# Columns loaded by halves, an identity kept in the transposed matrix, and VectorE's order: one core

## The chip, the cores and the metric

The kernel runs on 1 core of a Trainium2 chip. Its time is the device time of one execution, in microseconds (us). The engines are TensorE (PE in the profile, its weight loads PEld), VectorE (DVE), ScalarE (ACT), GpSimd (POOL) and SyncE (SP), which here only issues transfers. Each runs its own instructions in the order in which they are written, and waits on semaphores for the others.

## The reference

For each of 16 graphs there are `x` (1024 nodes x 256) and a weighted adjacency matrix `adj` (1024 x 1024). Four layers follow each other, each `x = layernorm(x + f(x, adj))`. Layer 0 touches 25 nodes a graph. The others, cut to what matters:

```python
# layer 1: attention
z = x @ W.T + bW;  e = leaky(ai(z) + aj(z).T, 0.2)
x = layernorm(x + softmax(where(adj > 0, e, -9e15), with a sink) @ z)
# layer 2
h = (1.0 + eps2) * x + adj @ x
x = layernorm(x + relu(h @ W1 + b1) @ W2 + b2)          # hidden 512
# layer 3
agg = eps3 * x + adj @ x
h = rmsnorm(agg @ W1 + b1) * rms_weight                  # hidden 1024
x = layernorm(x + silu(h) @ W2 + b2)
```

## The kernel before

A prologue (`prologue`) loads the weights and computes layer 0. Then `layers` takes the graphs one by one, and parts of the next graph's work are laid between those of the present one. Nothing is scheduled by a planner: every engine has a function `graph(b, ...)` whose text is its order. 1024 nodes are 8 tiles `k` (or `t`) of 128 and two halves `h` of 512. Where precision matters a float32 matrix is held as a sum hi + lo of two tiles of the type fp32r, and a product takes three matmuls: hi by hi, hi by lo, lo by hi.

- `agg_step(layer, k, h)` (L662 to L679) adds the contribution of node tile k to half h of the aggregate: 3 matmuls of 512 columns for each of two halves `d` of the features, 6 in all. The moving operand is the transposed matrix `mt_hi`, `mt_lo`: in layer 1 the attention weights (from `att`), in layers 2 and 3 the adjacency matrix. 16 such steps make a layer.
- The transposed adjacency matrix is made from column blocks. ACT issues `load_col` (L850): 1024 rows of 128 columns, 512 KB, into one of two slots of `adj_col` (`CR` = 2), after it has read the block before from that slot's transpose. POOL adds eps3 times the identity to the block's own 128x128 piece (`diagonal`, L1031). PE transposes it by 8 matmuls with the identity into two PSUM banks (`turn_col`, L638), ACT copies to `mt_hi` (`turn_hi`, L847), DVE subtracts to get `mt_lo` (`turn_lo`, L1095) and so frees the banks.
- Since eps3 is on that diagonal, layer 2 needs 1 + eps2 - eps3 more: in `agg_step` with `extra`, 3 matmuls of 128 columns with the tiles `cI2_hi`, `cI2_lo` for each `d` (L675 to L677).
- `attention_out` (L698) multiplies by W, `hidden_tile` (L713) by the first and `second_step` (L729) by the second weight matrix, `agg_hi` (ACT, L878) and `agg_lo` (DVE, L1109) take the aggregate out of PSUM as `a_hi`, `a_lo`. `residual`, `statistics`, `normalize` (DVE, L1120/L1125, L1137 to L1145, L1152) with `rstd_of` (POOL, L1009), `x_high` (ACT, L882) and `x_low` (POOL, L1014) are the way from a layer's output to the next layer's operand, by halves.
- `rms_sum` (L741) and `rms_row` (L753) on PE, with `mean_square` (L1219) and `rms_of` (L1035), make layer 3's norm. The second half of layer 3's second matmul (L729, 8 steps `m`) is done after half 0 of the next graph's layer 1.
- Attention weights of graph b + 1 are computed on DVE while PE is in layers 2 and 3 of graph b: `attention_sums` (L1160), `attention_columns`, `aj_rows` on PE (L649), `aj_copy` (L1102), then 8 times `scores` (mask L1182, L1184, L1189), each followed by `exp` on ACT (L886); `denominators` end it, and then `turn_att` (L629) transposes `att` on PE.
- SP stores the finished graph, loads the next one's `x` tiles and, once `att` has been transposed, its 8 rows of `adj` into `att` (512 KB each).

## Time and profile before

| | us |
|---|---|
| median of 3 runs (3111.78 to 3113.38) | 3112.48 |
| the profiled execution's own time | 3113.45 |
| its span on the chip | 3111.7 |
| PE busy | 2895.0 (93%) |
| DVE busy | 2082.6 (67%) |
| ACT busy | 1323.5 (43%) |
| POOL busy | 923.3 (30%) |

Busy time counts an engine's instructions, not its waits. Successive matmuls overlap in the profile, since the end of one is modelled: what a stream of them costs is read from start to start. "Idle before" is the time that an engine sat still before an instruction, and behind the arrow stands what ended it.

### The profile page before, as it was taken

What the parts mean: (1) busy time and instruction counts of PE and PEld (TensorE: products, weight loads), DVE (VectorE), ACT (ScalarE), POOL (GpSimd) and SP (SyncE); (2) the same over time, 40 slices, a digit from 0 to 9 for tenths busy, and PEclk for the clock granted to TensorE, in tenths of its full rate; (3) what the DMA queues carried; (4) which work ended last, traced back from release to release, by engine and by line L of the source; (5) the groups of instructions that cost most, each with busy time, mean ns of one, the idle gap of its engine ahead of it and who ended that gap; (6) DMA issues with size and microseconds to landing.
All of it is one profiled execution on the core that took longest, in us unless ns stands there. A gap on an engine that the chain in (4) does not pass through costs nothing.

```text
span 3111.7 us, 40093 instructions
## 1 busy us (share of the span) xinstructions
PE 2895.0 (93%) x14794; PEld 2438.7 (78%) x14794; DVE 2082.6 (67%) x4580; ACT 1323.5 (43%) x2468; POOL 923.3 (30%) x1088
## 2 busy tenths in 40 slices
PE   4729999999999999999999999999999999999997
PEld 4618888888888888888888888888888888888886
DVE  3277667685867758586776858676676858677533
ACT  0222634436253543535254453526344362635423
POOL 1113333242233224223322323233332422332230
PEclk8959999999999999999999999999999999999998
DMA  4023040211304030130403012040302103040100
GB/s 131 15 79 115 1 129 7 80 57 36 100 1 136 1 109 28 41 95 1 136 1 116 21 49 88 3 133 1 126 10 76 60 28 109 1 136 1 41 15 14
DMA packets 203442, 180.95 MB, mean 58 GB/s; under 512 B 15568, under 2 KB 184944, under 8 KB 203248
## 3 DMA queue, kind: packets, MB, share of 16 engines
q1 hardware_dynamic: 62560, 109.94, 10.3%
q10 hardware_dynamic: 140688, 68.46, 7.8%
q8 instruction: 118, 1.93, 0.3%
q14 instruction: 76, 0.62, 0.1%
HBM read 161.17 MB, written 17.19 MB: 57 GB/s over the span
## 4 chain that ended last, share of the span: by engine, by line
PE 77%; DVE 10%; ACT 3%; POOL 3%; issue 2%; DMA 0%; SPq 0%; ACTq 0%; POOLq 0%; DVEq 0%
PE bank L729 21%; PE bank L713 17%; PE bank L670 9%; PE bank L672 9%; PE bank L671 9%; PE bank L629 3%; PE bank L638 3%; DVE mt_lo L1095 3%; DVE stat L1137 2%; PE bank L698 2%; POOL x_lo L1014 2%; PE bank L753 1%; PE bank L741 1%; PE bank L649 1%; ACT mt_hi L847 1%
## 5 line engine op out<-in xcount | busy, mean ns | idle before, releaser
L729 PE MATMUL bank<-W,hid 128*128 128x256 f32 x3072 | 695.3, 380 | 5.9 <-ACT hid L922 5.9
L729 PEld LDWEIGHTS bank<-W,hid 128*128 128x128 f32 x3072 | 583.3, 190 | 97.5 <-issue 12.7
L670 PE MATMUL bank<-mt_hi,x_hi 128*128 128x512 f32 x1536 | 642.1, 418 | 0.0
L672 PE MATMUL bank<-mt_hi,x_lo 128*128 128x512 f32 x1536 | 606.0, 395 | 0.0
L671 PE MATMUL bank<-mt_lo,x_hi 128*128 128x512 f32 x1536 | 603.4, 393 | 0.0
L847 ACT ACTIVATE mt_hi<-bank 128x512 fp32r<-128x512 f32 x512 | 279.7, 600 | 583.2 <-PE bank L638 547.7
L1009 POOL TENSOR_TENSOR rstd<-ve,neg_half 128x4 f32<-128x4 f32 x128 | 130.2, 1017 | 908.3 <-DVE ve L1145 908.2
L1215 DVE TENSOR_TENSOR sq_sum<-sq_sum,scratch 128x512 f32<-128x512 f32 x224 | 155.1, 692 | 360.6 <-ACT scratch L917 360.6
L1095 DVE TENSOR_TENSOR mt_lo<-bank,mt_hi 128x512 fp32r<-128x512 f32 x512 | 329.8, 684 | 88.0 <-ACT mt_hi L847 86.2
L672 PEld LDWEIGHTS bank<-mt_hi,x_lo 128*128 128x128 f32 x1536 | 290.8, 189 | 65.5
L713 PE MATMUL bank<-a_hi,W_hi 128*128 128x512 f32 x768 | 332.1, 432 | 0.0
L670 PEld LDWEIGHTS bank<-mt_hi,x_hi 128*128 128x128 f32 x1536 | 292.8, 191 | 48.0 <-ACT scratch L917 4.2
L671 PEld LDWEIGHTS bank<-mt_lo,x_hi 128*128 128x128 f32 x1536 | 293.0, 191 | 44.6
L713 PE MATMUL bank<-a_hi,W_lo 128*128 128x512 f32 x768 | 303.6, 395 | 0.0
L713 PE MATMUL bank<-a_lo,W_hi 128*128 128x512 f32 x768 | 302.8, 394 | 0.0
L1014 POOL TENSOR_TENSOR x_lo<-x_even,x_hi 128x256 fp32r<-128x256 f32 x192 | 167.9, 885 | 286.1 <-ACT x_hi L882 286.1
L908 ACT ACTIVATE hid<-bank,b 128x512 f32<-128x512 f32 x256 | 176.0, 688 | 165.0 <-PE bank L729 127.1
L1014 POOL TENSOR_TENSOR x_lo<-x_odd,x_hi 128x256 fp32r<-128x256 f32 x192 | 165.8, 874 | 258.9 <-ACT x_hi L882 258.9
L886 ACT ACTIVATE att<-att,neg_top 128x1024 f32<-128x1024 f32 x128 | 147.1, 1151 | 211.3 <-DVE neg_top L1196 211.0
L922 ACT ACTIVATE hid<-hid 128x512 f32<-128x512 f32 x256 | 161.8, 632 | 160.9 <-DVE hid L1226 157.1
L1109 DVE TENSOR_TENSOR a_lo<-bank,a_hi 128x512 fp32r<-128x512 f32 x192 | 123.5, 685 | 153.5 <-ACT a_hi L878 153.5
L878 ACT ACTIVATE a_hi<-bank 128x512 fp32r<-128x512 f32 x192 | 103.1, 588 | 253.3 <-PE bank L672 253.3
(139 smaller groups left out, 4609.6 us busy)
## 6 DMA issues: line engine op xcount, KB each, us to landing
adj_col<-in_adj ACTq DMA_DIRECT2D x128, 512.0 KB, 3.9
att<-in_adj SPq DMA_DIRECT2D x128, 512.0 KB, 7.5
out<-x_even SPq DMA_DIRECT2D x64, 128.0 KB, 2.5
out<-x_odd SPq DMA_DIRECT2D x64, 128.0 KB, 1.9
x_even<-in_x SPq DMA_DIRECT2D x56, 128.0 KB, 4.9
x_odd<-in_x SPq DMA_DIRECT2D x56, 128.0 KB, 4.2
G<-in_L_gnn_W SPq DMA_DIRECT2D x2, 2560.0 KB, 14.8
W_f<-in_L_gnn_W SPq DMA_DIRECT2D x1, 1024.0 KB, 9.8
```

The source lines that it names most:

```text
L670: nc.tensor.matmul(dst[:], hi, mt_hi[:, k, cols], start=k == 0, stop=False)
L671: nc.tensor.matmul(dst[:], hi, mt_lo[:, k, cols], start=False, stop=False)
L672: mm = nc.tensor.matmul(dst[:], lo, mt_hi[:, k, cols], start=False, stop=done and not extra)
L713: mm = nc.tensor.matmul(hid_bank[i % 2][:], l[:, d, cols], r[:, d, :], start=(d == 0 and n == 0), stop=(d == DT - 1 and n == 2))
L729: mm = nc.tensor.matmul(out_bank[t // 2][:, t % 2 * D:(t % 2 + 1) * D], src[:, t * P:(t + 1) * P], W2[:, m, :], start=(m == 0 and t % 2 == ...
L847: nc.scalar.activation(mt_hi[:, k, i * HALF:(i + 1) * HALF], turn_bank[i][:], ACT.Copy)\
L886: nc.scalar.activation(att[:, t, :], att[:, t, :], ACT.Exp, bias=neg_top[:, t:t + 1], accum_out=total[:, t:t + 1]).then_inc(s_exp, 1)
L908: nc.scalar.activation(hid[:, m, :], src, ACT.Identity, bias=b13[:, m:m + 1])
L922: nc.scalar.activation(h_m, h_m, ACT.Silu).then_inc(s_silu, 1)
L1014: nc.gpsimd.tensor_tensor(x_lo[:, t, :], x_bufs[buf][:, t, :], x_hi[:, t, :].bitcast(F32), ALU.subtract).then_inc(s_x_lo, 1)
L1095: nc.vector.tensor_tensor(mt_lo[:, k, cols], turn_bank[i][:], mt_hi[:, k, cols].bitcast(F32), ALU.subtract).then_inc(s_turn_free[i], 1)
L1215: nc.vector.tensor_tensor(sq_sum[:], sq_sum[:], sq[:, m % 2, :], ALU.add).then_inc(s_sq_sum, 1)
```

## The change

Four things are done together.

1. `adj_col` gets a place for the whole matrix and lies in the same memory as `mt_lo`: a half block (k, h), 512 rows of 128 columns and 256 KB, is loaded into the place of `mt_lo[k, h]` once layer 1's step (k, h) has used it. SP issues these loads, 16 a graph, between its stores and loads. `turn_col(b, k, h)` transposes a half block (4 matmuls, one bank, the two banks by turns). Six of them stand in the loop of `second_step`, five in layer 1's half 1 (`COL_AT`), five in layer 2.
2. The diagonal now carries 1 + eps2 (`cI2`), and the matmuls L675 to L677 are gone. For layer 3 the 8 diagonal pieces are rewritten: DVE keeps each, plus (eps3 - 1 - eps2) times the identity, in `diag3`; once layer 2's half is summed, ACT writes the hi part (`diag_hi`) and POOL the lo part (`diag_lo`), 4 pieces in one instruction each.
3. `agg_done` is signalled for each `d`, and steps 6 and 7 of layer 3's half 1 are done first for d = 0, then for d = 1. `rms_sum` of half 1 has a bank of its own.
4. The orders of PE, ACT, POOL and DVE are rewritten to suit, and `score_mask` is cut out of `scores`.

```diff
     x_hi, x_lo = sb("x_hi", [P, NT, D], F32R), sb("x_lo", [P, NT, D], F32R)
     a_hi, a_lo = sb("a_hi", [P, DT, HALF], F32R), sb("a_lo", [P, DT, HALF], F32R)
@@ -484,12 +486,13 @@
 
     agg_pair = [banks[0:2], banks[2:4]]
     hid_bank = banks[0:2]
-    sum_bank, row_bank = banks[6], banks[2]
...
+
+    COL_AT = {0: (6, 0), 1: (7, 0), 4: (0, 1), 5: (1, 1), 6: (2, 1)}
...
+            def load_col(b, k, h):
+
+                if k < NT - 1:
+                    sp.wait_ge(s_att_used, used_count(b, k, h))
+                else:
+                    sp.wait_ge(s_agg, DT * agg_count(b, 1, h))
+                dst = adj_col[:, k, half_cols(h)].rearrange("p (t m) -> p t m", t=4)
+                src = adj[b, half_cols(h), k * P:(k + 1) * P].rearrange("(t p) m -> p t m", p=P)
+                sp.dma_start(dst, src).then_inc(s_col_in[k][h], 16)
...
+                for k in range(NT - 1):
+                    load_col(b, k, 0)
                 if not first:
...
+                load_col(b, NT - 1, 0)
+                if not last:
+                    load_xs(b + 1, tiles(0), 1 - buf, first)
                     sp.wait_ge(s_turned[1], turn_att_use(b, NT - 1) + 1)
                     for t in range(4):
                         load_row(b + 1, t)
+                for k in range(4):
+                    load_col(b, k, 1)
                 if not first:
                     for t in tiles(1):
...
+                for k in range(4, 6):
+                    load_col(b, k, 1)
+                if not last:
+                    load_xs(b + 1, tiles(1), 1 - buf, first)
+                for k in range(6, NT):
+                    load_col(b, k, 1)
...
+            def turn_col(b, k, h):
+                if k // 4 == h:
+                    pe.wait_ge(s_diag, b * NT + k + 1)
+                else:
+                    pe.wait_ge(s_col_in[k][h], (b + 1) * 16)
+                i = col_bank(k, h)
+                turn_free(i, turn_col_use(b, k, h))
+                src = adj_col[:, k, half_cols(h)]
+                for j in HALF_TILES:
+                    cols = slice(j * P, (j + 1) * P)
+                    mm = nc.tensor.transpose(turn_bank[i][:, cols], src[:, cols], ident[:])
+                mm.then_inc(s_turned[i], 1)
...
-                for d in range(DT):
+                if layer == 3 and k % 4 == 0 and k // 4 == h:
+                    pe.wait_ge(s_diag_lo, half_count(b, h))
+                for d in ds:
...
-                    mm = nc.tensor.matmul(dst[:], lo, mt_hi[:, k, cols], start=False, stop=done and not extra)
-                    if extra:
-                        own = dst[:, (k % 4) * P:(k % 4 + 1) * P]
-                        nc.tensor.matmul(own, hi, cI2_hi[:], start=False, stop=False)
-                        nc.tensor.matmul(own, hi, cI2_lo[:], start=False, stop=False)
-                        mm = nc.tensor.matmul(own, lo, cI2_hi[:], start=False, stop=done)
-                if k == NT - 1:
-                    mm.then_inc(s_agg, 1)
+                    mm = nc.tensor.matmul(dst[:], lo, mt_hi[:, k, cols], start=False, stop=done)
+                    if done:
+                        mm.then_inc(s_agg, 1)
+                if k < NT - 1 and layer == 1:
+                    mm.then_inc(s_att_used, 1)
...
                 pe.wait_ge(s_sq_sum, b * 2 * (HT3 - 1) + (h + 1) * (HT3 - 1))
-                out_free(b, 3, h, 0)
+                if h == 0:
+                    out_free(b, 3, 0, 0)
...
                 if not first:
                     for m in range(HT3):
                         second_step(b - 1, 3, 1, m)
-
+                        if m >= 2:
+                            turn_col(b, m - 2, 0)
+                else:
+                    for k in range(6):
+                        turn_col(b, k, 0)
                 for k in range(NT):
-                    agg_step(1, k, 1)
-                    if k % 2 == 1:
-                        turn_col(b, k // 2)
-                    if k == 3:
+                    agg_step(b, 1, k, 1)
+                    if k in COL_AT:
+                        turn_col(b, *COL_AT[k])
+                    if k == 2:
                         attention_out(b, 0, first)
-                for k in range(NT - 2):
-                    turned(turn_col_use(b, k))
+
+                def step_2(k, h):
+                    col_turned(b, k, h)
                     x_ready(b, 2, k)
-                    for h in range(2):
-                        agg_step(2, k, h)
-                        if k == 0 and h == 0:
-                            attention_out(b, 1, first)
-                    if k + 4 < NT:
-                        turn_col(b, k + 4)
-                    elif k == 5 and not last:
+                    agg_step(b, 2, k, h)
+
+                for k in range(4):
+                    step_2(k, 0)
+                    if k == 1:
+                        attention_out(b, 1, first)
+                    if k > 0:
+                        turn_col(b, k + 2, 1)
+                for k in range(4):
+                    step_2(k, 1)
+                    if k < 2:
+                        turn_col(b, k + 6, 1)
+                for k in range(4, NT):
+                    step_2(k, 0)
+                for k in range(4, NT):
+                    step_2(k, 1)
+                    if k == 4 and not last:
                         aj_rows(b + 1, False)
-                for h in range(2):
-                    for k in range(NT - 2, NT):
-                        turned(turn_col_use(b, k))
-                        x_ready(b, 2, k)
-                        agg_step(2, k, h)
...
+                for k in range(6, NT):
+                    agg_step(b, 3, k, 1, None, range(1))
                 rms_sum(b, 0)
-                agg_step(3, 7, 1)
+                for k in range(6, NT):
+                    agg_step(b, 3, k, 1, None, range(1, 2))
...
+            def diag_hi(b, h):
+
+                act.wait_ge(s_agg, DT * agg_count(b, 2, h))
+                for k in (4 * h + 2, 4 * h + 3):
+                    act.wait_ge(s_turn_free[col_bank(k, h)], turn_col_use(b, k, h) + 1)
+                nc.scalar.activation(diag_blocks(mt_hi, h), diag3[:, 4 * h:4 * h + 4, :], ACT.Copy).then_inc(s_diag_hi, 1)
...
+            def diag_lo(b, h):
+                pool.wait_ge(s_diag_hi, half_count(b, h))
+                nc.gpsimd.tensor_tensor(diag_blocks(mt_lo, h), diag3[:, 4 * h:4 * h + 4, :],
+                                        diag_blocks(mt_hi, h).bitcast(F32), ALU.subtract).then_inc(s_diag_lo, 1)
...
+                for h in range(2):
+                    diag_lo(b, h)
...
+            def turn_col_lo(b, k, h):
+                i, cols = col_bank(k, h), half_cols(h)
+                dve.wait_ge(s_turn_hi[i], hi_col_use(b, k, h) + 1)
+                if k // 4 == h:
+                    if b > 0:
+                        dve.wait_ge(s_diag_lo, half_count(b - 1, h))
+                    nc.vector.tensor_tensor(diag3[:, k, :], turn_bank[i][:, k % 4 * P:(k % 4 + 1) * P], gapI[:], ALU.add)
+                nc.vector.tensor_tensor(mt_lo[:, k, cols], turn_bank[i][:], mt_hi[:, k, cols].bitcast(F32),
+                                        ALU.subtract).then_inc(s_turn_free[i], 1)
```

PE, around the second matmul of layer 3's half 1. Before (L729 is `second_step`, L670 to L672 an aggregate step, L638 a turn):

```order
L729 MATMUL bank<-W,hid 128x256 [waits hidden_silu]
L729 MATMUL bank<-W,hid 128x256 x3
L670 MATMUL bank<-mt_hi,x_hi 128x512
L671 MATMUL bank<-mt_lo,x_hi 128x512
L672 MATMUL bank<-mt_hi,x_lo 128x512
...
L638 MATMUL bank<-ident,adj_col 128x128 [waits turn_bank_read0,diagonal_added]
L638 MATMUL bank<-ident,adj_col 128x128 x3
L638 MATMUL bank<-ident,adj_col 128x128 [waits turn_bank_read1]
L638 MATMUL bank<-ident,adj_col 128x128 x3
```

After (L780 is `second_step`, L689 a half turn; the last of these loops):

```order
L780 MATMUL bank<-W,hid 128x256 [waits hidden_silu]
L780 MATMUL bank<-W,hid 128x256 x3
L689 MATMUL bank<-ident,adj_col 128x128 [waits turn_bank_read0,diagonal_added]
L689 MATMUL bank<-ident,adj_col 128x128 x3
L780 MATMUL bank<-W,hid 128x256 [waits hidden_silu]
L780 MATMUL bank<-W,hid 128x256 x3
L689 MATMUL bank<-ident,adj_col 128x128 [waits turn_bank_read1,diagonal_added]
L689 MATMUL bank<-ident,adj_col 128x128 x3
...
L689 MATMUL bank<-ident,adj_col 128x128 [waits turn_bank_read0,adj_cols_loaded4_0]
```

A half turn follows each of the steps m = 2 to 7; before, the first turn came two aggregate steps after the loop.

DVE, from layer 2's second residual to the end of the scores. Before (`scores` 5 ahead of the residual L1125, `scores` 6 behind `normalize` L1152):

```order
L1182 TENSOR_SCALAR scratch<-att 128x1024 [waits masked,adj_rows_loaded5]
L1184 SCALAR_TENSOR_TENSOR att<-aj_row,shift 128x1024 [waits mask]
L1196 TENSOR_SCALAR neg_top<-top,floor 128x1 [waits masked,leaky]
L1189 ISA att,top<-att,scratch 128x1024
L1189 ISA top 128x1
L1125 TENSOR_TENSOR x_odd<-bank,x_odd 128x512 [waits bias_added_l1,out_bank_written] x2
...
L1152 TENSOR_SCALAR x_odd<-x_odd,mv,rstd 128x256 [waits rstd_l2]
L1152 TENSOR_SCALAR x_odd<-x_odd,mv,rstd 128x256 x3
L1182 TENSOR_SCALAR scratch<-att 128x1024 [waits masked,adj_rows_loaded6]
```

After (the residual is L1206, `normalize` L1233, the mask L1257, the rest of `scores` L1269 to L1281):

```order
L1206 TENSOR_TENSOR x_odd<-bank,x_odd 128x512 [waits bias_added_l1,out_bank_written] x2
...
L1226 TENSOR_SCALAR ve<-mv 128x4 [waits aggregates_l2]
L1257 TENSOR_SCALAR scratch<-att 128x1024 [waits masked,adj_rows_loaded5]
L1233 TENSOR_SCALAR x_odd<-x_odd,mv,rstd 128x256 [waits rstd_l2]
L1233 TENSOR_SCALAR x_odd<-x_odd,mv,rstd 128x256 x3
L1269 SCALAR_TENSOR_TENSOR att<-aj_row,shift 128x1024 [waits mask]
L1281 TENSOR_SCALAR neg_top<-top,floor 128x1 [waits masked,leaky]
L1274 ISA att,top<-att,scratch 128x1024
L1274 ISA top 128x1
L1257 TENSOR_SCALAR scratch<-att 128x1024 [waits masked,adj_rows_loaded6]
```

Row tile 5's scores now stand behind the residual, their mask in the place where DVE waits for POOL's `rstd`.

DVE, at the start of layer 1's half 1. After (L1190 is `agg_lo`, L1175 the copy of a diagonal piece, L1176 a half's lo part, L1218 `statistics` of the next graph's x):

```order
L1190 TENSOR_TENSOR a_lo<-bank,a_hi 128x512 [waits a_hi_ready] x2
L1175 TENSOR_TENSOR diag<-bank,gapI 128x128 [waits layer3_diagonal_lo,turn_bank_hi_taken0]
L1176 TENSOR_TENSOR mt_lo<-bank,mt_hi 128x512
L1175 TENSOR_TENSOR diag<-bank,gapI 128x128 [waits layer3_diagonal_lo,turn_bank_hi_taken1]
L1176 TENSOR_TENSOR mt_lo<-bank,mt_hi 128x512
L1218 BN_STATS stat<-x_odd 128x6 [waits x_loaded2,x_loaded3,x_loaded1,x_loaded0]
...
L1175 TENSOR_TENSOR diag<-bank,gapI 128x128 [waits layer3_diagonal_lo,turn_bank_hi_taken0]
L1176 TENSOR_TENSOR mt_lo<-bank,mt_hi 128x512
```

The lo parts of half blocks 2 to 5 stand behind the statistics, which wait for the next graph's x tiles; before, no turn's lo part did.

## Rows read from the trace of the kernel before

**Rows 1.** The page: busy us, share of the span, instructions.

```profile
PE 2895.0 (93%) x14794; PEld 2438.7 (78%) x14794; DVE 2082.6 (67%) x4580; ACT 1323.5 (43%) x2468; POOL 923.3 (30%) x1088
```

**Rows 2.** One graph's stretch: us, busy us (x) of PE, PEld, DVE, ACT, POOL; clock, DMA.

```profile
1293.40:1474.70 181.30, 175.95 (x908) 148.18 (x907) 129.30 (x283) 83.54 (x156) 57.98 (x67) 1.00 0.19 59
```

**Rows 3.** Waits of PE: us in total, times, longest.

```profile
PE bank L638 <- POOL adj_col L1031: 55.6, 45, 2.0
PE bank L753 <- DVE a_lo L1109: 11.0, 16, 1.5
PE bank L741 <- DVE x_odd L1125: 6.1, 8, 2.8
PE bank L741 <- DVE x_even L1125: 3.8, 8, 0.5
```

**Rows 4.** Timeline of PE, end of layer 2: start, duration, line.

```profile
1373.69 0.39 PE L670 MATMUL bank<-mt_hi,x_hi 128*128 128x512 f32 x1
...
1374.37 0.39 PE L670 MATMUL bank<-mt_hi,x_hi 128*128 128x512 f32 x1
...
1375.33 0.45 PE L670 MATMUL bank<-mt_hi,x_hi 128*128 128x512 f32 x1
...
1376.37 0.44 PE L670 MATMUL bank<-mt_hi,x_hi 128*128 128x512 f32 x1
```

**Rows 5.** Groups by line: count, busy us, mean ns.

```profile
L675 PE MATMUL bank<-cI_hi,x_hi 128*128 128x128 f32 x256 | 57.3, 224 | 0.0
```

**Rows 6.** Timeline of PE around a turn of layer 1's half 1.

```profile
1323.59 1.04 PE L638 MATMUL bank<-ident,adj_col 128*128 128x128 f32 x8
1324.38 0.48 PE L670 MATMUL bank<-mt_hi,x_hi 128*128 128x512 f32 x1
1324.70 0.39 PE L671 MATMUL bank<-mt_lo,x_hi 128*128 128x512 f32 x1
```

**Rows 7.** Timelines of POOL and of PE, the turn of column block 2.

```profile
1334.20 1.01 POOL L1009 TENSOR_TENSOR rstd<-ve,neg_half 128x4 f32<-128x4 f32 x1 [9.32 <-DVE ve L1145]
...
1335.69 1.09 PE L638 MATMUL bank<-ident,adj_col 128*128 128x128 f32 x8 [1.88 <-POOL adj_col L1031]
```

**Rows 8.** Timelines of DVE and PE, from layer 2's end to layer 3's hidden tiles.

```profile
1400.24 1.63 DVE L1184 SCALAR_TENSOR_TENSOR att<-aj_row,shift 128x1024 f32<-128x1024 f32 x1
1403.47 1.28 DVE L1125 TENSOR_TENSOR x_even<-bank,x_even 128x512 f32<-128x512 f32 x2
1421.39 1.28 DVE L1109 TENSOR_TENSOR a_lo<-bank,a_hi 128x512 fp32r<-128x512 f32 x2
...
1403.29 0.58 PE L670 MATMUL bank<-mt_hi,x_hi 128*128 128x512 f32 x1
1422.57 1.03 PE L629 MATMUL bank<-ident,att 128*128 128x128 f32 x8
```

**Rows 9.** Timelines of DVE and PE in layer 2, from `aj_copy` to the second hidden half.

```profile
1370.91 0.69 DVE L1102 COPY aj_row<-bank 128x512 f32<-128x512 f32 x1 [2.25 <-PE bank L649]
1374.26 1.28 DVE L1184 SCALAR_TENSOR_TENSOR att<-aj_row,shift 128x1024 f32<-128x1024 f32 x1
1388.26 1.28 DVE L1109 TENSOR_TENSOR a_lo<-bank,a_hi 128x512 fp32r<-128x512 f32 x2
...
1371.53 0.47 PE L670 MATMUL bank<-mt_hi,x_hi 128*128 128x512 f32 x1
1390.79 0.58 PE L713 MATMUL bank<-a_hi,W_hi 128*128 128x512 f32 x1
```

**Rows 10.** The page, DMA issues of the whole span: KB each, median us to landing.

```profile
adj_col<-in_adj ACTq DMA_DIRECT2D x128, 512.0 KB, 3.9
```

**Rows 11.** DMA issues of 1304 to 1311.

```profile
x_odd<-in_x SPq DMA_DIRECT2D x3, 128.0 KB, 6.8
```

**Rows 12.** Line L565, the loads of x tiles.

```profile
DMA to landing us min/median/max: 2.0/4.5/11.3
```

**Rows 13.** Groups by line on POOL.

```profile
L1014 POOL TENSOR_TENSOR x_lo<-x_even,x_hi 128x256 fp32r<-128x256 f32 x192 | 167.9, 885 | 286.1 <-ACT x_hi L882 286.1
```

271 lines of the change are left out of this document (139 added, 132 removed).

## The prediction

> **What bounds the kernel now.** I read the busy shares first. PE is busy 93% of the span [rows 1], and most of the rest is the prologue: in one graph of the steady part, 181.3 us long, it is busy 175.95 us, at a granted clock of 1.00, which is the 2.4 GHz level, while DVE is busy 129.3, ACT 83.5 and POOL 58.0 [rows 2]. So a graph costs what its matmuls cost, plus some 5 us in which PE waits. The table of PE's waits then says for whom: 55.6 us in 45 waits, three a graph, before a turn of a column block, 11.0 before `rms_row` (16 times), 6.1 and 3.8 before `rms_sum` [rows 3]. There is work to remove on PE itself and there are waits to remove; the question is whether DVE, whose orders change most, keeps up with a PE that comes sooner.
>
> **The matmuls that go.** The three identity matmuls of a (k, d) pair are not read from their durations, which overlap, but from the starts of the steps around them. Six 512-column matmuls in pairs of three without the extra ones: from 1373.69 to 1374.37, 0.68 us. With them: 1375.33 to 1376.37, 1.04 [rows 4]. The difference is 0.36, or 0.35 with the rounding of the starts, and 256 such triples run [rows 5]: 256 x 0.35 = 89.6 us. All of it is on PE's path.
>
> A triple has 384 columns. The Trainium skill ("TensorE: Matmul & The Clock Gate", Back-to-back issue gap) puts a matmul of 128 columns at about 56 ns by itself and about 81 in a stream with weight loads; by that the triples are worth 256 x 3 x 0.081 = 62 us as an estimate, and the forecast would be 27 us later. The trace disagrees, at 0.35 us a triple, and the trace decides.
>
> **The waits that go.** At the turn of block 2, POOL adds the diagonal only after a `rstd` that waits for DVE's variance, and PE sat 1.88 us [rows 7]. The halves have their own places now, loaded and given their diagonal far ahead, so this wait has no cause left: up to 55.6 us. What is late next there is layer 2's operand `x_lo`, see below. For `rms_row`, d = 0 of half 1 is now summed a full d earlier (two half steps of 0.68 each and `rms_sum` lie behind it), which is more than the longest wait, 1.5: 11.0 us. `rms_sum` of half 1 no longer waits for the residual: 9.9 us in rows, of which I leave out the one of 2.8, at the very end, where the residual is wanted soon after: 7.1 [rows 3]. Together with the matmuls: 89.6 + 55.6 + 11.0 + 7.1 = 163.3 us, 10.2 a graph.
>
> **What is added on PE.** Turns are cut in two. One of 8 transposes takes 0.79 us from start to the next step, whose first matmul then takes 0.32 to the next start where 0.23 is usual [rows 6]: 0.09 for the change of kind. Before there are 8 such changes a graph, after it 10, since six half turns lie among `second_step` matmuls that are plain float32 as they are. 2 x 0.09 x 16 = 3 us.
>
> **What is added elsewhere.** DVE copies 8 diagonal pieces a graph (128 x 128 out of PSUM, not in the trace): between nothing and the 0.69 of a 128 x 512 copy out of PSUM [rows 9]; I take 0.25, nearer to a quarter of its size, 2 us a graph. ACT has two more copies of 512 columns. POOL has two `diag_lo` of 128 x 512; its 128 x 256 subtraction takes 0.885 [rows 13], so between 0.9 and 1.8 each, and I take 1.5. ACT and POOL idle there. Loads of half a column block (256 KB) aren't in the trace: 512 KB land 3.9 us after their issue in the median [rows 10], 128 KB after 2.0 at best and 11.3 at worst [rows 12]. A half is wanted at the earliest four to five steps of 1.37 us and some turns after the step that frees it, 8 to 9 us; I take 4 and no wait, and keep 11.3 as the other end.
>
> **What is late next, place by place.** I laid the new orders out by hand, with PE's steps of 1.37 us and DVE's durations from the same trace.
>
> Tail of layer 3. DVE must finish the scores of 8 row tiles and `a_lo` before PE can start layer 3's hidden tiles. Before, `residual` starts at 1403.47 and `a_lo` ends at 1421.39 + 1.28 = 1422.67, PE's layer 3 starts at 1403.29 and after 14 steps is at its turn at 1422.57, wanting `a_lo` 0.79 later at 1423.36 [rows 6, 8]: 0.7 to spare. Now tile 5's scores, without their mask, stand behind the residual instead of ahead of it. That remainder takes 3.23 (1400.24 to 1403.47 [rows 8]), perhaps 2.7 where POOL leaves DVE alone; the mask is hidden in the wait for `rstd`. The residual can start as soon as its bank is written, as DVE has nothing else then, which gives 0.5 back. So `a_lo` is 2.3 later against PE: a wait of 1.6 us in each of 15 graphs, 24 us. Below: nothing, if the faster scores do more; above: 2.6.
>
> Layer 2's second hidden half. From the end of `aj_rows` PE took 1390.79 - 1371.53 = 19.3 us to it; it now has three plain steps there instead of four with extras (4.1 instead of 6.9): 16.5. DVE took from 1370.91 to 1389.54, 18.6 [rows 9], and loses one `a_lo` of 1.2 from that stretch: 17.4, begun 0.6 before, so it ends at 16.8. A wait of 0.3, and with `diag_lo` beside the scores I take 0.7: 10 us in 15 graphs, between nothing and 1.5 each.
>
> Layer 1 to 2. From `attention_out` of half 0 to the first step of layer 2 PE has five steps and three half turns, 8.5 us, and DVE, ACT and POOL need the same within half a microsecond, because DVE arrives there late: half blocks 2 to 5 wait behind statistics on x tiles that land 6.8 us after their issue [rows 11]. For this, for bank turns and for `aj` together 0.4 a graph: 6 us, between nothing and 2 each.
>
> First graph. There the next graph's x tiles are issued only behind its column halves, and the same statistics hold half block 2, so PE waits once for some 7 us (issue 1.5, landing 4.5, statistics 2), between 4 and 11.
>
> Sum of what is added: 3 + 24 + 10 + 6 + 7 = 50. The profiled execution's own time is 3113.45, 1 us above the median of the runs: 3113.45 - 163.3 + 50 = 3000.
>
> **Rivals.** (a) DVE hides it all: the waits that I price are differences of a few tenths between long sums. Then only the 3 and the first graph's 4 are added: 2957. For it: DVE is busy 129 us of 181 and gets its idle places filled; against it: the tail's order, which puts 3 us behind the residual whatever else happens.
>
> (b) DVE is the bound through layers 2 and 3. Every `diag_lo` that lies beside a score holds it, and DVE is then late at both places. The score line L1184 takes 1.28 us alone [rows 9] and 1.63 while POOL works [rows 8]. With 3 us more in 15 graphs: 3045. Against it: 0.35 an operation is what the rows show, and that is priced.
> The Trainium skill ("SBUF — State Buffer", Who interferes with whom) says that a DVE instruction with two inputs in SBUF and a GpSimd one that reads SBUF exclude each other for the whole instruction. By that rule two `diag_lo` can cost up to their full length, which is this rival and its 3 us; the rows bear out the contention and not the full length.
>
> (c) Slower than before: one queue on SP carries all, and its last column halves stand behind stores that wait for DVE and x loads that wait for the stores. POOL's `diagonal` 7 waits for the last half, and in POOL's order both `rstd` of layer 1's half 1 stand behind it, then `x_lo` 4 to 7, then PE. The half is issued when layer 1 ends, and POOL is wanted some 9 us later; from there each microsecond goes to PE. To eat 163 - 8 us it must land 10 us later than that in each of 15 graphs, 19 us after its issue: the longest landing of an x tile is 11.3 [rows 12]. Then 3115 and more.
>
> (d) No change at all: PE's path would have to be another engine's; the 5 us of waits in 181 exclude it but for a sum of (b) and (c).
>
> **How the numbers follow.** Forecast 50%, 2975 to 3025 by itself; (a) 25%; (b) 17%; (c) 3%, (d) 2%; 3% for a PE even quicker than (a), by waits in rows that I left. From (a) without its first-graph wait, 2950, to (b), 3045, the range holds 8 in 10 or somewhat more; I give 2947 to 3045. A change of less than 0.2%, 6 us, is what a measurement of this kernel can't tell from none. Faster by more: 95%; within: 2%; slower: 3%.
>
> **What would show it.** PE's matmul count falls by 768 to 14026, and its waits on POOL's `adj_col` vanish. The graph's period is 173 to 175 us; PE waits 1 to 2 us for `a_lo` or `exp` ahead of layer 3's hidden tiles and under 1.5 at layer 2's second half; once, in the first graph, several microseconds at the turn of block 4. DVE idles some 3 us ahead of layer 2's second residual. `rms_row` and `rms_sum` wait for nothing. The forecast is wrong if PE stands at `x_lo` or a turn in every graph, if column halves land later than 8 us, or if the step with its triple gone doesn't fall to 1.37 us.

## The result and the profile after

| | us |
|---|---|
| before, median of 4 runs | 3112.13 (3110.97 to 3113.38) |
| after, median of 4 runs | 3028.56 (3027.01 to 3030.10) |
| ratio, 95% interval | 0.9731 (0.9715 to 0.9748) |
| the profiled execution's own time, its span | 3028.88, 3027.1 |

Faster by 84 us, where 112 were forecast: inside the range, 29 above the forecast. First the page's busy line and the engines' shares of the chain that ended last, of the changed kernel; the third line is the chain of the kernel before.

```profile
PE 2807.9 (93%) x14026; PEld 2347.0 (78%) x14026; DVE 2104.3 (70%) x4707; ACT 1349.4 (45%) x2500; POOL 940.7 (31%) x1120
...
PE 46%; DVE 34%; issue 5%; DMA 4%; ACT 3%; POOL 2%; SPq 1%; DVEq 0%; POOLq 0%; ACTq 0%
```

```profile
PE 77%; DVE 10%; ACT 3%; POOL 3%; issue 2%; DMA 0%; SPq 0%; ACTq 0%; POOLq 0%; DVEq 0%
```

PE's busy time fell by 87 against [rows 1], its share stayed at 93%, and yet the chain runs through DVE for 34% instead of 10%. The busy line doesn't tell who bounds the kernel; the chain and the waits do. PE's waits in the changed kernel (total, times, longest), to set beside [rows 3]:

```profile
PE bank L702 <- DVE aj L1247: 59.7, 16, 32.1
...
PE bank L689 <- DVE mt_lo L1176: 27.4, 28, 8.8
PE bank L764 <- DVE a_lo L1190: 24.6, 28, 1.6
PE bank L780 <- ACT hid L987: 10.7, 16, 2.7
```

The waits for `adj_col` (55.6), for `rms_row` (11.0) and for the residual before `rms_sum` (9.9) are gone. New are waits for `aj` (59.7 less 32.1 in the prologue: 27.6), for free turn banks (27.4, of which 8.8 once in the first graph) and for `a_lo` (24.6, at two places of each graph). The wait for ACT's `hid` (10.7) was 5.9 before. One steady graph of PE in the changed kernel, the rows with the longest waits:

```profile
1150.91 0.63 PE L689 MATMUL bank<-ident,adj_col 128*128 128x128 f32 x4 [0.55 <-DVE mt_lo L1176]
1164.76 2.05 PE L702 MATMUL bank<-ident,aj 128*128 128x128 f32 x16 [1.85 <-DVE aj L1247]
1184.63 0.50 PE L764 MATMUL bank<-a_hi,W_hi 128*128 128x512 f32 x1 [1.18 <-DVE a_lo L1190]
...
1218.06 0.50 PE L764 MATMUL bank<-a_hi,W_hi 128*128 128x512 f32 x1 [0.68 <-DVE a_lo L1190]
```

What DVE does ahead of `aj` in that graph (its timeline, cut; between the rows shown it works without a pause), and POOL beside it:

```profile
1154.02 2.98 DVE L1233 TENSOR_SCALAR x_even<-x_even,mv,rstd 128x256 f32<-128x256 f32 x4
...
1158.62 0.84 DVE L1241 SCALAR_TENSOR_TENSOR sq_sum<-x_even,v_rows 128x256 f32<-128x256 f32 x1
...
1162.61 0.42 DVE L1241 SCALAR_TENSOR_TENSOR sq_sum<-x_even,v_rows 128x256 f32<-128x256 f32 x1
...
1163.08 1.36 DVE L1241 SCALAR_TENSOR_TENSOR sq_sum<-x_even,v_rows 128x256 f32<-128x256 f32 x1
...
1164.48 0.23 DVE L1247 TENSOR_SCALAR aj<-qj,c_cols 128x8 f32<-128x8 f32 x1
```

```profile
1152.41 2.94 POOL L1083 TENSOR_TENSOR x_lo<-x_odd,x_hi 128x256 fp32r<-128x256 f32 x4 [1.36 <-ACT x_hi L947]
1155.31 6.50 POOL L1089 TENSOR_TENSOR x_odd<-x_odd,b_row 128x256 f32<-128x256 f32 x8
1162.78 1.37 POOL L1103 TENSOR_TENSOR mt_lo<-diag,mt_hi 128x512 fp32r<-128x512 f32 x1 [0.97 <-ACT mt_hi L943]
```

An attention sum takes 0.42 us while POOL is idle, 0.84 beside its bias additions and 1.36 beside `diag_lo`. The kernel before had the same stretched sums, but DVE had time for them: there `aj` was ready at 1367.06 and PE took it at 1369.77, 2.7 us later. Behind `aj` DVE did one more lo part, up to 1368.66, and then stood idle for the 2.25 us of [rows 9].

```profile
1366.83 0.23 DVE L1166 TENSOR_SCALAR aj<-qj,c_cols 128x8 f32<-128x8 f32 x1
...
1367.38 1.28 DVE L1095 TENSOR_TENSOR mt_lo<-bank,mt_hi 128x512 fp32r<-128x512 f32 x2
```

The graph's repeat, from one row of `aj` to the next on PE (before, then after): 178.85 and 174.59 us. Over 14 repeats the means are 179.0 (295.41 to 2801.93) and 174.2 (292.44 to 2730.81).

```profile
1190.92 0.55 PE L649 MATMUL bank<-ident,aj 128*128 128x128 f32 x3
...
1369.77 0.44 PE L649 MATMUL bank<-ident,aj 128*128 128x128 f32 x2
```

```profile
1339.35 0.49 PE L702 MATMUL bank<-ident,aj 128*128 128x128 f32 x2 [1.85 <-DVE aj L1247]
```

So 14 x 4.9 = 68 us were won in the steady part and the other 16 in the first and last graph and the prologue.

### The profile page after: what moved, and what is told of

It reads as the page before. It is cut to its first block, busy times and chain, and to the rows that moved or that the text cites. A ratio compares the mean times of both kernels' runs of the same rounds, so it can differ in the third digit from the quotient of the medians.

```text
span 3027.1 us, 39239 instructions
## 1 busy us (share of the span) xinstructions
PE 2807.9 (93%) x14026; PEld 2347.0 (78%) x14026; DVE 2104.3 (70%) x4707; ACT 1349.4 (45%) x2500; POOL 940.7 (31%) x1120
## 3 DMA queue, kind: packets, MB, share of 16 engines
q8 instruction: 113, 1.85, 0.3%
## 4 chain that ended last, share of the span: by engine, by line
PE 46%; DVE 34%; issue 5%; DMA 4%; ACT 3%; POOL 2%; SPq 1%; DVEq 0%; POOLq 0%; ACTq 0%
PE bank L764 15%; PE bank L780 14%; DVE att L1269 5%; DVE att L1274 4%; DVE stat L1218 4%; DVE sq_sum L1241 4%; PE bank L724 3%; PE bank L726 3%; PE bank L725 3%; PE bank L675 3%; DVE mt_lo L1176 2%; DVE scratch L1257 2%; DVE x_even L1233 2%; DVE x_odd L1233 2%; DVE a_lo L1190 2%
## 5 line engine op out<-in xcount | busy, mean ns | idle before, releaser
L780 PE MATMUL bank<-W,hid 128*128 128x256 f32 x3072 | 707.9, 381 | 10.7 <-ACT hid L987 10.7
L780 PEld LDWEIGHTS bank<-W,hid 128*128 128x128 f32 x3072 | 578.7, 191 | 97.1 <-issue 17.0
L724 PE MATMUL bank<-mt_hi,x_hi 128*128 128x512 f32 x1536 | 632.5, 412 | 0.0
L764 PE MATMUL bank<-a_hi,W_hi 128*128 128x512 f32 x768 | 331.1, 431 | 24.6 <-DVE a_lo L1190 24.6
L919 ACT ACTIVATE mt_hi<-bank 128x512 fp32r<-128x512 f32 x256 | 152.5, 596 | 416.7 <-PE bank L689 416.7
L1078 POOL TENSOR_TENSOR rstd<-ve,neg_half 128x4 f32<-128x4 f32 x128 | 141.3, 1104 | 604.8 <-DVE ve L1226 604.2
L973 ACT ACTIVATE hid<-bank,b 128x512 f32<-128x512 f32 x256 | 176.0, 688 | 184.0 <-PE bank L780 130.4
L764 PEld LDWEIGHTS bank<-a_hi,W_hi 128*128 128x128 f32 x768 | 144.7, 188 | 80.6 <-DVE a_lo L1190 33.6
L960 ACT ACTIVATE hid<-bank,b 128x512 f32<-128x512 f32 x128 | 88.2, 689 | 264.2 <-PE bank L764 264.2
L1190 DVE TENSOR_TENSOR a_lo<-bank,a_hi 128x512 fp32r<-128x512 f32 x192 | 124.9, 683 | 101.3 <-ACT a_hi L936 101.2
```

Source lines behind the costliest of these rows:

```text
L724: nc.tensor.matmul(dst[:], hi, mt_hi[:, k, cols], start=k == 0, stop=False)
L764: mm = nc.tensor.matmul(hid_bank[i % 2][:], l[:, d, cols], r[:, d, :], start=(d == 0 and n == 0), stop=(d == DT - 1 and n == 2))
L780: mm = nc.tensor.matmul(out_bank[t // 2][:, t % 2 * D:(t % 2 + 1) * D], src[:, t * P:(t + 1) * P], W2[:, m, :], start=(m == 0 and t % 2 == ...
L919: nc.scalar.activation(mt_hi[:, k, half_cols(h)], turn_bank[i][:], ACT.Copy).then_inc(s_turn_hi[i], 1)
L973: nc.scalar.activation(hid[:, m, :], src, ACT.Identity, bias=b13[:, m:m + 1])
L1190: nc.vector.tensor_tensor(a_lo[:, d, :], agg_pair[h][d][:], a_hi[:, d, :].bitcast(F32), ALU.subtract).then_inc(s_a_lo, 1)
```

## The experiments

Chips differ by 3 us, so each time is to be compared by its ratio to the kernel before on the same chip. "Against after" is the difference of the ratios times 3112. A ratio is known to 5 us on either side and such a difference to some 7, so that the -9 is hardly more than none.

| run | us | ratio (95%) | against after |
|---|---|---|---|
| after | 3028.56 | 0.9731 (0.9715 to 0.9748) | |
| before, without the triples | 3074.64 | 0.9882 (0.9865 to 0.9898) | |
| after, triples back | 3042.86 | 0.9778 (0.9764 to 0.9793) | +15 |
| after, no layer 2 bias additions | 2989.67 | 0.9605 (0.9591 to 0.9620) | -39 |
| after, layer 3 in whole steps | 3041.15 | 0.9773 (0.9758 to 0.9787) | +13 |
| after, other order ahead of `aj` | 3016.38 | 0.9690 (0.9675 to 0.9704) | -13 |
| after, `a_lo` before score 3 | 3021.49 | 0.9703 (0.9688 to 0.9717) | -9 |
| after, no diagonal copies | 3014.97 | 0.9681 (0.9665 to 0.9697) | -16 |
| four orders together | 2983.01 | 0.9580 (0.9566 to 0.9594) | -47 |
| second set of orders | 2987.17 | 0.9594 (0.9579 to 0.9608) | -43 |
| the same and POOL's move | 2959.43 | 0.9504 (0.9488 to 0.9520) | -71 |
| the same, triples back | 3016.57 | 0.9689 (0.9675 to 0.9704) | -13 |
| the same, `a_lo` before the denominators | 2949.59 | 0.9478 (0.9464 to 0.9491) | -79 |

**The triples in the old schedule.**

```diff
-                extra = layer == 2 and k // 4 == h
+                extra = False
```

> The kernel before with layer 2's three extra identity matmuls a (k, d) pair left out (its layer 2 lacks the term (1 + eps2 - eps3) x), all orders as before. It prices the triples in the old schedule. Theory A (each triple is 0.35 us of PE's path, and DVE keeps up): 256 x 0.35 = 89.6 us less, 3022 to 3028, and no wait of PE that was not there before grows by over 5 us. Theory B (DVE becomes the bound once layer 2 is 5.6 us shorter, the same that the changed kernel shows at aj): PE's wait ahead of the aj rows or of a_lo grows by 1 to 3 us a graph, 3038 to 3070. If the triples are worth 0.24 us each, 62 us in all, 3050 with no such wait.

It gained 37 us of the 89.6. PE's waits in it, to compare with [rows 3]:

```profile
PE bank L638 <- POOL adj_col L1031: 68.5, 44, 2.0
...
PE bank L713 <- DVE a_lo L1109: 12.4, 15, 0.9
PE bank L649 <- DVE mt_lo L1095: 12.4, 15, 1.0
```

12.9 more at the turns, and two new waits for DVE of 12.4 each: 37.7 given back. (The wait at L649, the aj rows, is for the lo part behind `aj`, not for `aj` itself.) Theory A falls; B holds in kind, 5 us above its range. So even the old orders leave DVE late once layer 2 is shorter; none of the new DVE or POOL work is needed for it.

**The triples in the changed kernel.** The edit takes the second part of the change back: `cI3` on the column diagonal, L675 to L677 of the kernel before again, and out go

```diff
-                diag_hi(b, 0)
-                        diag_hi(b, 1)
-                    diag_lo(b, h)
-                    nc.vector.tensor_tensor(diag3[:, k, :], turn_bank[i][:, k % 4 * P:(k % 4 + 1) * P], gapI[:], ALU.add)
```

> The changed kernel with the second part undone: eps3 on the column diagonal, the 256 triples back in layer 2, no copy of the diagonal pieces, no diag_hi and diag_lo; columns still by halves, DVE's new order kept. Theory A (the mis-sized term is DVE's lateness against a PE that comes 5.6 us sooner): the triples cost 89.6, and the waits for aj (26 us) and for a_lo of layer 2's second half (about 18) go or nearly go with them, 3070 to 3085. Theory B (the waits have their cause elsewhere and stay): 3118. Waits for a_lo at the tail of layer 3 stay in both, at about 0.7 a graph.

15 us slower, 27 below what A allowed; neither range holds the time. The chain and PE's waits of this run:

```profile
PE 76%; DVE 11%; DMA 3%; ACT 3%; issue 2%; POOL 1%; SPq 1%; DVEq 0%; POOLq 0%; ACTq 0%
```

```profile
PE bank L705 <- DVE aj L1245: 31.9, 1, 31.9
...
PE bank L692 <- DVE mt_lo L1174: 14.4, 9, 9.0
PE bank L771 <- DVE a_lo L1188: 10.9, 16, 0.9
```

Against the changed kernel 27.6 us of waits for `aj` are gone, 13.7 for `a_lo` and 13.0 at turns: 54, so that A's waits went as it said, and those at turns besides. Its steady repeat is 174.5 us (296.79 to 2740.24 in 14), against 174.2. In the steady graphs the second part of the change, forecast at 5.6 us of matmuls in each, earned 0.4.

**POOL beside the sums.**

```diff
-                for t in range(NT):
-                    add_bias(b, 1, t, buf)
-                    dve.wait_ge(s_bias[layer - 1], b * NT + t + 2)
+                    if layer == 2:
+                        dve.wait_ge(s_x_lo, x_count(b, 1, t + 1))
+                    else:
+                        dve.wait_ge(s_bias[layer - 1], b * NT + t + 2)
```

> The changed kernel without POOL's eight additions of layer 2's bias row (leaves out b22), which run beside DVE's attention sums. Theory A (POOL beside DVE stretches the sums from 0.42 to 0.84 us and so makes aj late): the eight or so stretched sums fall to 0.42 to 0.5 each, aj comes 2.5 to 4 us sooner, PE's 1.85 us wait at the aj rows falls to under 0.3, and the time is 3000 to 3006. Theory B (the eight copies of diagonal pieces, or DVE's order by itself, make it late): aj comes less than 1 us sooner, 3018 to 3029.

39 us faster, 10 more than A's end. On DVE's timeline all eight sums take 0.42, and the normalize beside `x_low` 2.12 instead of 2.98:

```profile
1142.34 2.12 DVE L1234 TENSOR_SCALAR x_even<-x_even,mv,rstd 128x256 f32<-128x256 f32 x4
...
1148.44 0.42 DVE L1242 SCALAR_TENSOR_TENSOR sq_sum<-x_even,v_rows 128x256 f32<-128x256 f32 x1
```

The waits for `aj` (27.6 us in the steady graphs) are gone, and 3.3 at turns; most of the rest goes with TensorE's clock, see the last section. The removal also took `diag_lo` away from beside the last sum, so this run doesn't tell apart the two pieces of POOL's work.

**Layer 3 in whole steps.**

```diff
-                for k in range(6, NT):
-                    agg_step(b, 3, k, 1, None, range(1))
+                agg_step(b, 3, 6, 1)
                 rms_sum(b, 0)
-                for k in range(6, NT):
-                    agg_step(b, 3, k, 1, None, range(1, 2))
+                agg_step(b, 3, 7, 1)
```

and one bank for both `rms_sum`, with the residual ahead of `mean_square` again.

> The changed kernel with the third part undone: steps 6 and 7 of layer 3's second half whole again with rms_sum between them, and rms_sum of half 1 in the shared bank, behind the residual. Theory A (as the forecast has it, 11.0 us at rms_row and 7.1 at rms_sum come back): 3044 to 3050. Theory B (half of it is hidden, since DVE, and with it PE's wait for a_lo, is late there anyway): 3034 to 3040. Under 3032 would mean that this part is worth nothing.

13 us, 3041 and so between the two. The waits for the residual came back whole (6.1 and 3.7 us). At `rms_row` only 1.2 came back, not 11.0. This run kept the signal for each d, and ACT now copies d = 0 while PE sums d = 1: the copy starts 0.60 us before PE's last step ends, in the kernel before 0.03 behind it. From `rms_sum` to `rms_row` PE takes 4.04 us before, 3.43 in this run and 3.25 in the changed kernel (means of 14 graphs), so 0.6 a graph went with the signal (this run's other orders differ from the kernel before as well) and 0.2 with the split into d. Other waits of the table fell by 10 us in this run (3.5 for `hid`, 3.5 at turns, 2.2 for `sq_sum`, 1.1 for `a_lo`), so the table accounts for 1 of the 13; what the other 12 are stays open.

**The order ahead of `aj`.** After the residual of layer 1's second half DVE takes blocks 3 and 4, the next graph's normalize, block 5, one sum tile, the statistics, a second sum tile, block 6, the normalize, block 7, and the last two sum tiles.

```diff
+                turn_col_lo(b, 4, 1)
+                if not last:
+                    normalize(b + 1, 0, 1, 1 - buf)
+                turn_col_lo(b, 5, 1)
+                if not last:
+                    attention_sums(b + 1, range(4, 5), 1 - buf)
                 statistics(b, 1, 1, buf)
-                turn_col_lo(b, 4, 1)
-                turn_col_lo(b, 5, 1)
+                if not last:
+                    attention_sums(b + 1, range(5, 6), 1 - buf)
+                turn_col_lo(b, 6, 1)
                 normalize(b, 1, 1, buf)
...
```

> The changed kernel with another order of DVE ahead of aj: the next graph's second normalize and two of its four attention sums come before and around the statistics of layer 1's second half, so that they run before POOL's x_low and bias additions begin (ACT turns block 6 before its x_high for it). Nothing is left out. Theory A (contention with POOL made aj late): normalize falls from 2.98 to about 1.4 us, two sums from 0.84 to 0.42 each, aj comes 2.5 to 4 us sooner, PE's wait for it (1.85 us, and 0.3 between its two banks) is gone: 2998 to 3006. Rival B (the contention only moves to other operations): less than 8 us gained, over 3020. Rival C (x_lo of layer 2's tiles 4 to 7 comes 3 to 4 us later and PE now stands there): above 3028.

What A and what C described both happened, and the time lies in no one's range: below C's 3028, above A's 3006. `aj` is in time (one wait left, in the prologue) and the waits at turns fell by 11.2 us, but PE now stands at `x_lo`, in 15 graphs:

```profile
PE bank L724 <- POOL x_lo L1083: 27.6, 15, 2.0
```

**`a_lo` before the scores of tile 3.**

```diff
-                    for t in range(4):
+                    for t in range(3):
                         scores(b + 1, t)
                 agg_lo(b, 2, 1)
+                if not last:
+                    scores(b + 1, 3)
```

> The changed kernel with DVE's a_lo of layer 2's second half ahead of the scores of tile 3 instead of behind them. Theory A (PE's 1.18 us wait there is DVE's order alone): the wait goes, 15 x 1.2 = 18 us, and nothing comes back, 3009 to 3013. Rival B (ACT's a_hi isn't there yet, or the later exp of tile 3 is given back at the tail of layer 3, where a_lo waits for DVE's scores): 3018 to 3028.

The wait went (a_lo 24.6 to 11.9 us, with hardly more at the tail), yet only 9 us were gained. Neither reason of B holds: most of the difference went with the clock, as the last section shows.

**Without the diagonal copies.**

```diff
+                    if b == 0:
-                    nc.vector.tensor_tensor(diag3[:, k, :], turn_bank[i][:, k % 4 * P:(k % 4 + 1) * P], gapI[:], ALU.add)
+                        nc.vector.tensor_tensor(diag3[:, k, :], turn_bank[i][:, k % 4 * P:(k % 4 + 1) * P], gapI[:], ALU.add)
```

> The changed kernel in which DVE copies the diagonal pieces in the first graph alone (leaves out layer 3's own diagonal in the other 15). It takes 8 x 0.29 = 2.3 us a graph off DVE. With the triples put back the time was only 14 us higher, so something costs about 75 us of their 89.6. Theory A (the copies are a good part of it, since DVE has no idle time from layer 1's first output to aj): aj comes 1 to 1.5 us sooner, and the waits at turns (about 1.3 us a graph more than without the second part) fall to half or less, 2990 to 3005. Rival B (PE alone, coming sooner, meets a DVE that is late by its old work): under 8 us gained.

16 us, between the theories: 6.4 less at `aj`, 7.8 less at turns, 4.1 more for `a_lo`, and none of the clock dips of the last section. The copies are a part of DVE's lateness and not the greater one.

**All orders together.** The two edits above, the scores of tile 5 before layer 2's second residual, where DVE idled 3.26 us, and in the first graph

```diff
                     sp.wait_ge(s_y[0], NT)
+                    load_xs(b + 1, range(NT), 1 - buf, True)
                 for k in range(NT - 1):
```

> Nothing left out: the order ahead of aj as in the other run, a_lo ahead of the scores of tile 3, the scores of tile 5 before the second residual of layer 2 (where DVE idles 3.3 us), and the next graph's x tiles loaded before the column halves in the first graph. If the waits are independent their gains add: about 28 at aj, 18 at layer 2's second half, 10 at the tail of layer 3, 8.8 in the first graph, together 65, so 2963, between 2955 and 2975. If DVE is the bound over the whole graph, so that a wait that goes comes back elsewhere, less than half of it: above 2995.

47 of 65, between the two outcomes that were expected. The 8.8 of the first graph and both waits for `a_lo` are gone; the 27.3 at `x_lo` account for the shortfall.

**The second set, with and without POOL's move.** DVE's statistics come right behind block 4 and all sums last, and half block 2 before the statistics that wait for x tiles:

```diff
+                turn_col_lo(b, 4, 1)
                 statistics(b, 1, 1, buf)
-                turn_col_lo(b, 4, 1)
                 turn_col_lo(b, 5, 1)
+                if not last:
+                    normalize(b + 1, 0, 1, 1 - buf)
                 normalize(b, 1, 1, buf)
...
```

POOL's move:

```diff
                     rstd_of(b + 1, 0, 1)
+                for t in tiles(0):
+                    add_bias(b, 1, t, buf)
                 rstd_of(b, 1, 1)
                 for t in tiles(1):
                     x_low(b, 1, t, buf)
-                for t in range(NT):
+                for t in tiles(1):
                     add_bias(b, 1, t, buf)
```

> Nothing left out. The four orders of the run before, but DVE takes the statistics of layer 1's second half right after block 4, the next graph's normalize in the wait for rstd, and all four attention sums last; POOL adds layer 2's bias to tiles 0 to 3 before rstd instead of beside the sums; and DVE's half block 2 comes before the statistics that wait for x tiles. That run still had a 1.8 us wait for x_lo in each of 15 graphs (27.3 us) and 10.3 at turns. If POOL's shorter stay beside the sums lets aj come in time: 2983 - 27 - 8 = 2948, 2940 to 2956. If DVE is late for aj again (the wait only changes its name): over 2965.

> The same without POOL's move: all eight bias additions again behind x_low of layer 1's second half, beside DVE's attention sums. Theory A (contention): the sums that run beside POOL take 0.84 instead of 0.42, about eight instead of four, so aj comes 1.5 to 2 us later and PE waits 1 to 1.5 us a graph for it: 15 to 22 us more than with the move, 2963 to 2970. Theory B (POOL's place doesn't matter): within 4 us of it.

POOL's move is worth 28 us: four additions run where DVE reads PSUM or has one input alone (they take 2.84 us there, the four beside the sums 3.56). Theory A, more strongly than forecast. Without it, 16.5 us of waits for `aj` are back, and 10.9 for a relu of ACT. With it, this is left of PE's longer waits (that for `aj` is the prologue's alone); `a_lo` at the tail is late again, so DVE is still the bound there, and 2948 was 11 too low:

```profile
PE bank L704 <- DVE aj L1251: 32.0, 1, 32.0
...
PE bank L766 <- DVE a_lo L1194: 11.0, 16, 0.8
PE bank L782 <- ACT hid L989: 10.8, 16, 2.7
```

> The run with all orders and POOL's move, with the second part undone (256 triples of identity matmuls back, no diagonal copies, no diag_hi and diag_lo). In the changed kernel the triples' return cost 14 us. Theory A (they are 0.33 to 0.35 us each on PE, and it was DVE's lateness that took their place in the changed kernel): where DVE keeps up they cost nearly all of 85 to 90 us, so 75 to 90 more than without them, 3025 to 3038. Theory B (PE hides most of a 128-column matmul with its load behind 512-column ones, and a triple is worth 0.05 to 0.1 us): 15 to 25 more.

57 us more, between the theories. The run with triples has no wait for `a_lo` (0.4 us in all), the one without has 11.0. So the triples take 57 + 11 = 68 us of PE's path.

**`a_lo` before the denominators.**

```diff
+                    sink_args(b + 1)
+                agg_lo(b, 3, 0)
+                if not last:
                     denominators(b + 1)
-                agg_lo(b, 3, 0)
```

and on ACT `agg_hi(b, 3, 0)` between the exps of tiles 6 and 7.

> Nothing left out. As the run with all orders and POOL's move, and at the tail of layer 3 DVE takes a_lo of half 0 before the softmax denominators, where it sat 1.11 us for ACT's exp of the sink; ACT takes a_hi between the exps of tiles 6 and 7. In that run PE still waited 0.70 us a graph for this a_lo (11.0 us in 16 waits). Theory A (the wait is this order): a_lo comes 1.5 us sooner, the wait goes, and PE instead waits 0.2 to 0.4 us for the exp of tile 7, 4 to 6 us in all: 2959 - 11 + 5 = 2953, 2948 to 2956. Rival B (whatever PE gains is given back at aj, where DVE was 0.2 us late already): within 3 us of 2959.

Theory A: 2949.59, 0.9478 (0.9464 to 0.9491) of before, the fastest of all and 79 below the changed kernel. DVE has `a_lo` ready before PE's turn is done, and PE's rows show no wait:

```profile
1180.26 1.27 DVE L1196 TENSOR_TENSOR a_lo<-bank,a_hi 128x512 fp32r<-128x512 f32 x2
```

```profile
1181.80 1.06 PE L677 MATMUL bank<-ident,att 128*128 128x128 f32 x8
1182.62 0.48 PE L766 MATMUL bank<-a_hi,W_hi 128*128 128x512 f32 x1
```

## Why the prediction was right, and where it was not

**The waits that go** held: `adj_col` 55.6, `rms_row` 11.0 and `rms_sum` 7.1 to 9.9 us are not in the table. For `rms_row` the reason given was mostly wrong: 0.6 of the 0.8 us a graph are gone without the earlier sum of d = 0, in the run that kept only the signal for each d.

**The matmuls that go** came out too high, and above all were not banked. What one triple costs, measured by the start of the last 512-column matmul ahead of it and the start of what follows, is 0.517 against 0.227 us in the median, 0.29; the next 512-column matmul starts its successor 0.28 later instead of 0.23, but 47 of 256 triples of the kernel before have none behind them. That is 0.33 at most, 85 us; the three pairs of runs, with the waits that came or went and the clock dips of the last section, give 57 + 11 = 68, 15 + 54 + 8 = 77 and 37 + 38 + 3 = 78 us. I take 75 below. The 0.35 of [rows 4] was read from one step, which has this later start as well.

The estimate by the Trainium skill ("TensorE: Matmul & The Clock Gate", Back-to-back issue gap), 62 us, was about as far off on the other side: a triple takes 0.29 us and by that section 0.24.

**What is late next** is the term that failed. "For this, for bank turns and for `aj` together 0.4 a graph: 6 us, between nothing and 2 each" measured 27.6 at `aj` and 18.6 at banks (27.4 less 8.8), 46 us, above its upper end of 30. This place was the one that the working didn't lay out in microseconds: "For this, for bank turns and for `aj` together" is all it says. Laid out from layer 1's second attention output, it comes out. The rows of PE that start that output, before and after:

```profile
1344.06 0.33 PE L698 MATMUL bank<-WT_hi,a_hi 128*128 128x256 f32 x1
```

```profile
1141.81 0.39 PE L749 MATMUL bank<-WT_hi,a_hi 128*128 128x256 f32 x1
```

From there PE reached the aj rows in 25.7 us (1369.77); now it would in 21.1 (1164.76, less the 1.85 of waiting), 4.6 sooner. Ten triples, 3 us, stood in that stretch, and its turns, four whole ones before and five halves now, take 1.3 less. DVE has `aj` ready 23.0 us behind the same start before and 22.9 after: it comes to layer 1's residual later (4.0 us behind that start instead of 1.7), and its chain from there is 2.3 shorter. So 4.6 us were asked for, 2.7 were free, and the 1.85 was left as a wait. The means over 15 graphs say the same: 4.7 sooner, 2.6 free, 1.84 waited. The 2.25 of [rows 9] is not this slack. In 1.1 of it PE works on the aj rows, and the other 1.1 lies between the lo part at 1368.66 and PE; that is why PE without its triples waited there for the lo part, 0.83 a graph.

The other terms:

| term | forecast | measured |
|---|---|---|
| turns in halves | 3 | 0 |
| tail of layer 3, `a_lo` | 24 | about 11 (0.68 a graph) |
| layer 2's second half | 10 | about 14 (1.18 a graph) |
| first graph | 7 | 8.8 |
| `aj` and turn banks | 6 | 46 |
| second step's `hid` | none | 5 (5.9 to 10.7) |
| start up to `aj` in the prologue | none | -5 (36.8 to 32.1) |

Turns take 7.0 us of a graph in both kernels: eight of 0.79 and 0.09 behind each before; now eleven halves of 0.355 and 0.09, and five among the `second_step` matmuls of 0.44 with nothing behind them.

The tail was overpriced in three places. From the start of layer 2's second residual to the end of `a_lo` DVE took 19.2 us before and 21.4 after (1196.58 to 1218.00), 2.2 more and not 2.7. The residual starts 0.5 us ahead of PE's layer 3 where it started 0.2 behind, 0.2 more than was given back. And PE wants `a_lo` 20.3 us after that start instead of 20.1. The lateness at `aj` has no part in it: the runs in which PE doesn't wait there, the one with the triples back and the second set with POOL's move, wait as long for this `a_lo` (10.9 and 11.0 us in 16).

Added up: 3113.45 - 75 - 55.6 - 11.0 - 9.9 + 11 + 14 + 8.8 + 46 + 5 - 5 = 3042, less 1.7 for one clock dip fewer, 3040, where 3029 stands. I could not place the 11 us between. The same sum for the run with the triples back, with its own waits (14.4 at turns, 10.9 for `a_lo`) and six dips fewer, gives 3052 where 3043 was measured, so most of it isn't the price of the triples. Set against the forecast, the waits at `aj` and turns put it off by 40 us and the triples by 15, while the overpriced tail (13), the turns (3) and the 11 unplaced ones took part of that back. That it is 29 off and not 55 is luck.

**The rivals.** (b) had the right mechanism, DVE as the bound and POOL holding it, with the wrong place and mostly the wrong POOL work: not `diag_lo` beside the scores at the tail, but `add_bias` beside the attention sums, and one `diag_lo` beside the last of them, by the 0.94 us which that sum takes longer. The rule of the Trainium skill that it leaned on ("SBUF — State Buffer", Who interferes with whom, and in full under SBUF: two separate sides) bore on the bound after all, at a place that I had not looked at. It says exclusion for the whole instruction: a sum (0.42) and an addition (0.71, a quarter of the 2.84 that four took where DVE read PSUM or one input) in turn would need 1.13 a pair. The rows show a pair each 0.88 (from one sum's start to the next), so a doubling of the sum, less than the rule says. Beside `diag_lo` it is nearer to the rule: over 1.07 us of overlap the sum took 0.94 longer. (a), "DVE hides it all, 2957", is what the changed kernel becomes after its orders are mended: 2959 and 2950. (c) is refuted: 256 KB halves land 3.0 us after their issue in the median,

```profile
adj_col<-in_adj SPq DMA_DIRECT2D x256, 256.0 KB, 3.0
```

the slowest 5.2, and PE waits for none. POOL's `diagonal` stood 28.5 us for them in 28 waits, and its `rstd` behind them then still waited for DVE in the graph shown above (1.21 us).

**The signs.** The count of 14026, the vanished waits on `adj_col`, DVE's 3 us of idle time before layer 2's second residual (3.26) and the first graph's wait at block 4 came as said. The wait ahead of layer 3's hidden tiles, 0.68 us, was to be 1 to 2. And one of the signs of a wrong forecast came: PE stands at a turn in nearly every graph (16.9 us in 25 waits between 400 and 2900 us). The period of 173 to 175 came too, but by luck: [rows 2] is 181.3 long, 2.3 longer than the repeat of 179.0. From 179.0 the forecast's own terms lead to 179.0 - 10.2 + 2.8 = 171.6, and 174.2 was measured.

## What to carry to other kernels

When work is taken off the engine that is busy 93%, read first, at every hand-over, how long the other engine's result lies ready before this one takes it: that slack, here 2.7 us a graph at `aj`, is about the most that can be earned ahead of it before the bound changes hands. The idle time which follows in the other engine's rows, here 2.25, also holds this engine's own work. The gain that doesn't show isn't lost: it is bought back by moving the other engine's work ahead of its due places, and by moving a third engine's work away from beside it, here another 79 us without one instruction less. Price a removed instruction by taking it out of more than one schedule, since its worth was 15 us in one, 37 in another and 57 in the third, for a price of some 75 on PE's path.

## What the runs showed of the hardware that was not expected

PE's own waits can cost more than they last: TensorE's clock can fall right behind one. In the run with `a_lo` before score 3, PE waited 1.83 us for `aj` and then worked at a lower granted clock (windows of 2 us; the clock is the third number from the end):

```profile
1161.00:1163.00 2.00, 2.00 (x15) 2.00 (x16) 1.97 (x6) 0.00 (x0) 0.00 (x0) 0.86 0.00 0
1163.00:1165.00 2.00, 2.00 (x7) 1.61 (x7) 2.00 (x5) 0.00 (x0) 0.00 (x0) 0.50 0.00 0
1165.00:1167.00 2.00, 2.00 (x8) 1.58 (x7) 1.82 (x3) 0.00 (x0) 0.00 (x0) 0.78 0.00 0
```

0.50 is the 1.2 GHz level, and its matmuls of 512 columns start 0.43 apart instead of 0.23. By these rows the dip costs 0.28 + 1.00 + 0.44 = 1.7 us. Between 400 us and 2900 us the traces have 6 such dips before, 8 in it without the triples, 5 after and 5 with layer 3 in whole steps, 10 in this run, and 6 and 5 in the two where PE waits for `x_lo`. Each of these 45 begins within 1.5 us after the end of a wait of 1.80 to 2.01 us. The seven other runs have none; their longest wait there was 1.4 us. The mean granted clocks agree: 0.977 to 0.978 in the executions of the changed kernel, 0.980 to 0.981 without the bias additions. So the missing bias additions gained 8.5 of their 39 us by the five dips, and the missing diagonal copies as much.

The run with the earlier `a_lo` lost 8.5 us by five more dips in the profiled execution, whose mean clock was 0.974. Its others had 0.976 to 0.977. One dip lowers the mean by 0.0006, so those had two or three more than the changed kernel, 3 to 5 us as an estimate; with the 12.7 us of waits that went, this fits the 9 that were measured. Whether a 1.85 us wait brings a dip changes from graph to graph with nothing else different in the rows; what decides it was not tried.
